# Attention tiles in falling order of width, and a fourth buffer for the first x tiles

## The reference

```
x = x + attn(layernorm(x), Wk, Wq, Wv)
    K, Q, V = x@Wk, x@Wq, x@Wv;  scores = Q K^T / 32, causal
    attn = softmax(scores) @ V
x = x + ffn(layernorm(x), weight_q, weight_scale, bias)
    amax = max|x| of the row;  x_scale = max(amax, 1e-6) / 127
    x_q = clip(round(x / x_scale))            # int8
    out = (x_q @ weight_q^T) * x_scale * weight_scale + bias
```

## Time and profile before

| what | us |
|---|---|
| two timed runs | 536.6 and 588.92, median 562.76 |
| the profiled execution | 535.71 |
| its span, slowest core (core 6) | 534.1 |
| spans of the eight cores | 528.6 to 534.1 |
| PE busy in the span | 399.1 |
| DVE busy | 249.1 |
| ScalarE busy | 172.9 |
| first Q matmul | 38.67 |
| end of phase 2 (last V matmul) | 240.4 |

### The profile page before, as it was taken

The page is one execution under the profiler, slowest core; times in us unless marked ns, Lnnn a source line. Parts: engine busy times, 40 slices in busy tenths (PEclk is TensorE's granted clock), DMA queues, the critical chain, the costliest instruction groups (busy, mean ns, idle before and its releaser), DMA issues.

```text
span 534.1 us, 6028 instructions; the slowest of 8 cores (528.6 to 534.1 us)
## 1 busy us (share of the span) xinstructions
PE 399.1 (75%) x2008; PEld 188.2 (35%) x2008; DVE 249.1 (47%) x425; ACT 172.9 (32%) x321; POOL 82.9 (16%) x47
## 2 busy tenths in 40 slices
PE   0129994499969999993646866779888988987644
PEld 0114442244434444441223323334444444443211
DVE  3234447644444344335465445565565545545320
ACT  4443006830020000003442345434565355245220
POOL 4000000000000000002133122333131322111311
PEclk9999997599979999996688779899999999999867
DMA  7999902510000000006022112222202220220101
GB/s 162 194 197 199 239 2 81 151 46 0 1 0 1 0 2 0 1 0 196 1 79 79 40 40 79 80 79 80 64 21 75 80 80 0 80 79 1 40 16 62
DMA packets 11454, 35.08 MB, mean 66 GB/s; under 512 B 896, under 2 KB 896, under 8 KB 11424
## 3 DMA queue, kind: packets, MB, share of 16 engines
q1 hardware_dynamic: 6480, 23.60, 13.8%
q0 software_dynamic: 4944, 11.11, 11.1%
HBM read 31.56 MB, written 8.39 MB: 75 GB/s over the span
## 4 chain that ended last, share of the span: by engine, by line
PE 59%; DVE 17%; issue 8%; DMA 7%; ACT 7%; DVEq 1%; POOLq 0%; POOL 0%; ACTq 0%; SPq 0%
PE psF L197 32%; PE psF L500 10%; PE psF L607 9%; PE psF L374 7%; DMA xbuf<-x 6%; DVE st L413 2%; DVE x L615 2%; DVE st L385 2%; DVE st L541 2%; ACT xqf L587 2%; DVE st L393 1%; DVE st L259 1%; DVE t L523 1%; DMA xr<-x 1%; DVE st L417 1%
## 5 line engine op out<-in xcount | busy, mean ns | idle before, releaser
L500 PE MATMUL psF<-wqt_sb,xqT 128*128 128x512 bf16 x256 | 72.3, 446 | 38.5 <-ACT xqT L463 25.6
L607 PE MATMUL psF<-Vt,AT_sb 128*128 128x512 bf16 x272 | 63.8, 390 | 18.4 <-DVE t L523 11.3
L197 PE MATMUL psF<-xnT,wq_sb 128*128 128x512 bf16 x256 | 62.9, 411 | 7.1 <-DVE xnT L283 7.1
L374 PE MATMUL psF<-KT,QT 128*128 128x512 bf16 (+3 forms) x320 | 62.6, 352 | 0.9 <-DVE Vt L212 0.9
L527 POOL TENSOR_TENSOR outf<-t,x1b 128x1024 f32<-128x1024 f32 x16 | 37.7, 2353 | 143.5 <-DVE t L523 143.5
L197 PE MATMUL psF<-wv_sb,xnT 128*128 128x512 bf16 x256 | 55.9, 379 | 0.0
L197 PE MATMUL psF<-xnT,wk_sb 128*128 128x512 bf16 x256 | 55.9, 379 | 0.0
L500 PEld LDWEIGHTS psF<-wqt_sb,xqT 128*128 128x128 bf16 x256 | 27.4, 111 | 78.4 <-issue 60.5
L241 PE MATMUL psBF<-ident_sb,xnbuf 128*128 128x128 bf16 x128 | 13.4, 273 | 47.2 <-ACT xnbuf L233 43.9
L622 POOL TENSOR_TENSOR x1b<-x,bb_sb 128x1024 f32<-128x1024 f32 x16 | 37.6, 2352 | 70.4 <-DVE x L615 60.9
L476 ACT ACTIVATE A_sb<-psF,st 128x1024 bf16<-128x1024 f32 (+7 forms) x16 | 14.9, 932 | 100.8 <-DVE st L424 100.8
(11 more groups left out here) (60 smaller groups left out, 373.5 us busy)
## 6 DMA issues: line engine op xcount, KB each, us to landing
xr<-x SPq DMA_DIRECT2D x16, 512.0 KB, 5.0
y<-outf SPq DMA_DIRECT2D x16, 512.0 KB, 3.6
xbuf<-x SPq DMA_DIRECT2D x13, 512.0 KB, 4.5
wq_sb<-wq POOLq DMA_DIRECT2D x1, 2048.0 KB, 25.2
wk_sb<-wk POOLq DMA_DIRECT2D x1, 2048.0 KB, 42.2
wv_sb<-wv POOLq DMA_DIRECT2D x1, 2048.0 KB, 56.7
wqt_sb<-wqt POOLq DMA_DIRECT2D x1, 2048.0 KB, 61.1
xbuf<-x POOLq DMA_DIRECT2D x3, 512.0 KB, 6.3
```

The lines of the kernel that those rows point to most:

```text
L197: (lambda t: t.matmul(psQ(b), lhsT, rhs, start=st, stop=sp)))()
L374: (lambda te: te.matmul(score_ap(b, n), lhsT, rhs, start=st, stop=sp)))()
L500: (lambda te: te.matmul(psMM[:, sl * 512:(sl + 1) * 512], xqT[jpar][:, kc * 128:(kc + 1) * 128], wqt[:, kc * D + sl * 512: kc * D + (sl + ...
L607: fn = (lambda jj=jj, sl=sl, st=st, sp=sp: (lambda te: te.matmul(psMM[:, sl * 512:(sl + 1) * 512], AT_sb[:, jj * 128:(jj + 1) * 128], Vt[: ...
```

## The change

Two things. In phase 1 there are four x buffers instead of three; the first four x tiles come by GpSimd's queue ahead of the weights, and a later tile waits for the tile four back. In phase 3 the tiles are taken in falling order: pass i works on tile `order[i] = 15 - i`, so its number of key blocks falls from 16 to 1. Buffers, semaphores and the pass structure still go by i.

```
-    xbuf = [at(f"xbuf{i}", [128, D], F32) for i in range(3)]
+    xbuf = [at(f"xbuf{i}", [128, D], F32) for i in range(4)]
...
-        for t0 in range(3):
+        for t0 in range(4):
             m_dx[t0] = sch.op("gpsimd",
...
-                xpar = t % 3
+                xpar = t % 4
                 stt = st1[t % 4]
-                if t >= 3:
-                    w = [("ss", m_xn[t - 3]), ("vs", m_red[t - 3])]
+                if t >= 4:
+                    w = [("ss", m_xn[t - 4]), ("vs", m_red[t - 4])]
...
+        order = list(range(NT - 1, -1, -1))
         for it in range(NT + 2):
             i = it
             h = it - 1
             j = it - 2
+            ti = order[i] if i < NT else -1
+            tj = order[j] if 0 <= j < NT else -1
...
-            nch = i + 1
+            nch = ti + 1
...
-                                 dma(xr[par][:], x_h[i * 128:(i + 1) * 128, :]),
+                                 dma(xr[par][:], x_h[ti * 128:(ti + 1) * 128, :]),
...
-                    lhsT = QT[:, kc * S + i * 128: kc * S + (i + 1) * 128]
+                    lhsT = QT[:, kc * S + ti * 128: kc * S + (ti + 1) * 128]
...
-                                    dma(y_h[j * 128:(j + 1) * 128, :], outf[jpar][:]),
+                                    dma(y_h[tj * 128:(tj + 1) * 128, :], outf[jpar][:]),
```

More of the change, by code:

```diff
@@ L23 @@
 ENGINES = ("sync", "gpsimd", "tensor", "vector", "scalar")
-SEMS = ("dx0", "dx1", "dx2", "dp0", "dp1", "dp2", "dr0", "dr1", "do0", "do1",
+SEMS = ("dx0", "dx1", "dx2", "dx3", "dp0", "dp1", "dp2", "dp3",
+        "dr0", "dr1", "do0", "do1",
         "dwi", "dwq", "dwk", "dwv", "dwt", "dwm", "dws", "dwb",
@@ L232, in build_nc @@
                 m_b2 = sch.cnt["ss"]
-                m_xn[h] = sch.op("scalar", (lambda par=par, hx=h % 3, stt=stt: (lambda s: s.activation(
+                m_xn[h] = sch.op("scalar", (lambda par=par, hx=h % 4, stt=stt: (lambda s: s.activation(
                     xnbuf[par][:], xbuf[hx][:], AF.Identity,
@@ L403, in build_nc @@
             if i < NT:
-                diag = (psF1[:, i * 128:(i + 1) * 128] if i < 8
-                        else psF2[:, (i - 8) * 128:(i - 7) * 128])
+                diag = (psF1[:, ti * 128:(ti + 1) * 128] if ti < 8
+                        else psF2[:, (ti - 8) * 128:(ti - 7) * 128])
                 w = [("ts", m_sc[i]), ("dwm", m_mask)]
```

## The result

The changed kernel takes 552.81 us (median), the kernel before 536.09 in the eight runs that now exist of it: a ratio of 1.032 with a 95% interval of 1.030 to 1.034. It is slower by 16.7 us, 3.2%; forecast were 551.0 us and a range of 543 to 557. The 562.76 us that stood as the median of before came of two runs, and one of them, 588.92, was of a kind that comes up now and then here, with the cores of one die at a lower granted clock and a longer time: ratios and intervals leave such runs out, medians have them in, which moves a median by at most 0.4 us. The comparison with 536.6 was the right one.

What follows compares the result with a forecast made beforehand. Prediction: FFN latency loop bounds narrow tiles; scores, softmax and AV in a row bound wide ones. 20.6 (reversal) - 4.35 - 0.95 (fourth buffer) = +15.3 us on span 534.1, plus 1.6: 551.0 us, range 543 to 557.

Steps and rivals of the forecast that it cites:

- the head: Phase 3's first two passes, without FFN: 16 and 15 blocks replace one and two, 23.3 + 21.0 + 4.0 - 15.6 = +32.7 us.
- the tail: Last two attention passes, with FFN: two blocks and one replace 15 and 16, 32.8 - 44.9 = -12.1 us.
- PE is the bound in wide tiles: Rival: FFN holds AV up, so each wide pass without it shrinks by 6.0 us; 535.0 us, not slower; chance 0.05.
- The clock stays up: Rival: no clock loss in phase 3's first two and last two passes, 4.0 and 3.6 less, 543.4 us; chance 0.18.
- The low clock lasts longer: Rival, phase 3: 2.8 us more in first passes, 2.2 in last, 1 to 2 in the middle, 557.5; chance 0.10.
- The weights don't gate: Rival, phase 1: PE doesn't wait for the weights, 4.8 us less, 546.2 us; chance 0.12.
- the prefetch gives nothing: Rival, phase 1: x tiles ahead of the weights hold wv up, 4.35 us more, 555.4 us; chance 0.05.
- The clock's 4.0: Phase 3's first two passes: PE idles about 5.9 us before A's transposes, lowering its clock, 2.0 us lost in each.
- Phase 1, -5.3: Fourth buffer: V of the first batch starts 4.35 us sooner, the gap after that batch shrinks by 0.95.
- The gap after the first batch: Second gap of phase 1: ScalarE's 0.62 and 0.33 us waits for x loads go, -0.95 us.
- the two sums: Phase 1 counts of weights and x tiles landing between wq, wk and wv, giving 1.7 us per x tile, 13.6 per weight.
- the other value, 1.8 us more: Phase 1: if PE's 2.6 us wait before K lowers the clock, V starts at 66.2 and the term is -2.5.

Runs made afterwards that it cites:

- with the clock held: For the way to AV: changed kernel with 26 extra matmuls per head pass, 548.21 us; for the 14.6 us pass: narrow passes and drain filled too, 531.38 us.
- the fill that brought 3.1 us in the head: Changed kernel with 26 extra matmuls in each of the two passes without FFN, filling PE's whole gap before the transposes: 548.21 us, ratio to before 1.024.
- four buffers alone: Changed kernel with the tiles in rising order, keeping the four x buffers and four preloads: 531.88 us, ratio to before 0.994.
- the filled head: Changed kernel with 16 extra matmuls in each of the two passes without FFN, filling part of PE's gap: 552.86 us, ratio to before 1.032.
- the rising kernel: Rising order, four x buffers, with 9 to 22 extra matmuls in PE's gaps in passes of 2 to 8 blocks and the drain: 516.41 us, ratio 0.964.

## Why the forecast came out as it did

**The mechanism held, and the size within 2 us; part of the agreement is luck.** 20.6 us for the reversal were forecast, 20.5 measured alone; -5.3 for the fourth buffer, -4.2 measured alone; +15.3 in all, +16.1 between the two spans and 16.7 between the medians. Two terms of the reversal were wrong by as much in opposite directions: the head by -1.25 us, the tail by +1.3. Of the rivals, "PE is the bound in wide tiles" is out: with no FFN in it the way from scores to AV took 8.27 us against 8.24, and 7.86 with the clock held (248.86 and 250.72 above), where this rival had the whole pass 6.0 us shorter. "The clock stays up" is out by the 1.87 us transposes and by the fill that brought 3.1 us in the head. "The low clock lasts longer" came true in the tail alone. "The weights don't gate" and "the prefetch gives nothing" are both out, by the waits for wq and wk and by the -4.2.

**Taken against the median of two runs** that was given as the time before (562.76), the forecast of 551.0 would read as a gain. It was made against 536.6, and said so, with slower at 0.67; eight runs of before give 536.09. It is by this base, and not by a wait or a path, that the forecast and the measured loss could be read as opposite.

**The steps that failed are three terms of the sum.**
- The tail, "2 x 16.4 = 32.8", measured 34.10. The nearest row was the first pass with an FFN in the kernel before; its FFN took 5.38 us. The three passes after it took 16.7, 16.9 and 17.0 us, and their average stood in the prediction ("16.7 each"). In the last two passes of the change the FFN took 6.06 and 6.07, which lay within the stated 35.0. With the clock held a pass takes 14.6.
- The head, +32.7, measured +31.45. The clock's 4.0 was right for PE: transposes 0.8 us longer in each pass, AV 0.8 and 1.6. But it was added to the path as a whole, and only 3.1 of it reached the path. With full-speed transposes AV started 7.86 and 7.73 us after the scores, with the slow ones 8.27 and 7.95: of 1.6 us in the transposes 0.6 counted. The 8.24 that stood for this way had ScalarE's normalised row (L537, until 492.67 in the kernel before) ahead of the copy of the transposes, which the first head pass doesn't have, so part of the delay was in it already.
- Phase 1, -5.3, measured -4.3 between the two slowest cores. wq was put at 31.7 and came at 35.0 there (first Q at 32.3 to 35.1 over the cores). V was put 4.35 sooner, at 64.4; it came at 67.28, 1.5 sooner than the 68.75 of before. Over all cores it was 64.3 to 67.5 in place of 66.8 to 68.8, and 62.8 to 64.5 with four buffers alone. The gap after the first batch shrank by 1.5 instead of 0.95, from 21.7 us to 20.2, and the last 1.3 are Q batches that ran faster (15.27 and 15.99 us where before they took 16.08 and 16.41), a time that varies between 14.5 and 16.6 over the cores of both kernels. So -4.3 is nearer to the forecast than its parts are. K's wait, 2.6 forecast, was 2.46 on the slowest core and 0.6 to 2.5 over all. Nothing measured the 1.7 us of an x tile and the 13.6 of a weight apart; the two sums also left out wqt, which landed 5.3 us behind wv before, and the counts of x tiles that were to come sooner (1.6, 2.2 and 1) were given without a row.

**The clock after K's wait.** The forecast charged nothing for 2.6 us of idling, because 3.16 us of it had left the next matmuls at full speed. The K matmuls after 2.46 us did run at full speed (64 in 13.97 us, as without a wait); the other value, 1.8 us more, didn't come. But the reason didn't carry: the trace of before has a shorter gap with a slow FFN behind it, in the pass of 8 blocks, and the changed kernel has both cases too.

```profile
343.74 5.30 PE L500 MATMUL psF<-wqt_sb,xqT 128*128 128x512 bf16 x16 [2.56 <-DVE st L413]
```

```profile
393.32 5.30 PE L504 MATMUL psF<-wqt_sb,xqT 128*128 128x512 bf16 x16 [2.57 <-DVE st L417]
426.51 3.61 PE L504 MATMUL psF<-wqt_sb,xqT 128*128 128x512 bf16 x16 [3.43 <-ACT xqT L467]
```

The granted clock was 0.68 over the first two of these and 1.00 over the third. In the filled head 2.55 us of idling after 16 matmuls also went with a slow AV. So the length of one gap doesn't tell whether the next matmuls are slow; what else decides it isn't shown here.

## What to carry to other kernels

Before reordering a software pipeline, write down which passes lack which stage: the passes at the ends of the loop should get the work that hides nothing, here the narrow tiles, because a stage is free only beside a tile wide enough to cover it. A prefetch ahead of the bulk loads of weights pays only until the weights become late; holding back the tiles that aren't needed yet was worth 3.2 us on top of the 4.2 of the extra buffer. Where PE waits in a latency loop, useless matmuls that fill the gap to its end can be worth more than either: 15.5 us here. A term that is taken from one row should be held against its neighbours: here three more rows of the kind stood beside it, each slower.

## What the hardware showed

A fill that ended 2.2 to 2.6 us before the next useful matmuls left AV slow on seven of eight cores in the first pass and on six in the second, and gave nothing in the time; one that ended at most 0.4 us before them left it at full speed on all eight and gave 3.1 us in the head. Gaps of 2.56 and 2.57 us stood before FFNs of 5.30 us, gaps of 3.16 and 3.43 before FFNs of 3.61. In the narrow passes and the drain of the rising kernel, 9 to 22 extra matmuls each raised the mean granted clock of a core from about 0.92 to 0.965. They did not hold the FFN up: in the pass of three blocks it still started 0.70 us after the fill's end, when its own operand came.
